# Two score banks become three shared ones, side products get two banks and are evicted one step later

## The chip, the cores and the metric

One core of a Trainium2 chip. The metric is the device time of one execution in microseconds; lower is better. Engine names: PE is TensorE (PEld its weight loads), DVE is VectorE, ACT is ScalarE, POOL is GpSimd, SP is SyncE, which here only issues DMAs.

## The reference

16 sequences of 1024 tokens pass one layer. The parts that matter:

```python
h = tok_ref(x)      # embedding, 128x128 projection, 6 gated convolutions (3 taps), projection
# differential attention, 8 heads of 16 channels:
attn1 = softmax(q1 k1^T / 4);  attn2 = softmax(q2 k2^T / 4)
gate_in = window_stats(attn1), window_stats(attn2)  # windows of 4 rows: mean, std(ddof=1), max, min
alpha = sigmoid(relu(relu(gate_in gw1 + gb1) gw2 + gb2) gw3 + gb3)
h = h + (alpha attn1 + (1 - alpha) attn2) v Wo
# feed-forward on layernorm(h): normalised once more inside, attn_w, then one expert per
# sequence (fc1, gelu, fc2), next projection, gelu
h = h + ffn_ref(layernorm(h))
```

The score matrices are 1024x1024, 16 of them (8 heads, two attentions) for each sequence; row maximum, row minimum and sum of squares of every row feed the window statistics.

## The kernel before

Sixteen bodies, one for each sequence, run in a loop over groups of eight. A body has 128 steps (STEPS); a unit (one head of one attention) takes 8 of them, so step n works on unit n // 8, row tile n % 8. The engines run through the steps in a fixed order, each on its own, tied by semaphores:

- PE: scores(n) (two 512-column halves into ps_s), weighted(n) (exps times v into ps_o), scores_t(n) (the transposed scores of 12 steps earlier into ps_t), then the side products that the plan puts into step n, each into a bank of ps_w.
- DVE: row_max(n) (L726, reads ps_s, writes neg_s and the row maximum), the unit's collection of ps_o if there is one, row_min(n-1) (L734), then the side tasks of the step.
- ACT: exp_t(n) (L594, reads ps_t), the side tasks of the step (evictions of ps_w among them), squares(n) (L587, reads neg_s).
- POOL: only side tasks, in the order of the plan. SP: DMA issues in a hand-written order.

The side work of the sequence before (attention output, gate, layer norms, experts) and of the sequence after (embedding, convolutions, projections for q, k, v) is cut into tasks; plan() puts each into a step, with at most one side product per step. COST is PE's price of a task, POOL_COST that of POOL in tenths of a microsecond, STEP_WEIGHT what POOL works off per step, GAP and SPREAD the least distance to the task before. A task of engine X is done when its last instruction raises side_X; later tasks wait for counts of that semaphore, and every POOL task also waits for the POOL task before it (wait_own).

PSUM has 8 banks. Before: ps_s four (two tiles of two banks, tile n in pair n % 2, free again after row_max(n-2)), ps_t two, ps_o one, ps_w one. A side product waits until the product before it is evicted, and is evicted in its own step: ACT after exp_t(n), DVE after row_min(n-1).

Three chains around the change. msplit j (POOL, 4 small instructions in step 8j-2) splits the row maxima of a unit; mrow j (DVE, at the end of step 8j) waits for it, and DVE's row_max(8j+1) stands behind mrow. snap (POOL, step 16, 11.3 us) takes the statistics; unit 2's collection on DVE in step 21 waits for its end. qk (POOL) splits q and k into three bf16 parts; load_unit on SP then copies the parts of a head into qst and kst, twelve DMAs of 32 KB, and scores of the unit's first step waits for all of them (s_ring). After the last body a tail without scores does the side work of the last sequence, one task after another.

## Time and profile before

| | us |
|---|---|
| runs before | 5776.51, 5781.32, 5792.61 (median 5781.32) |
| the profiled execution | 5777.35, its span 5775.5 |
| prologue, up to the first row_max | 138.2 |
| first to last of 16 body starts | 5182.1 (15 bodies, mean 345.5) |
| last body and tail | 455.2 |
| PE busy | 5177.0 (90%) |
| ACT busy | 5196.2 (90%) |
| DVE busy | 5109.5 (88%) |
| POOL busy | 2454.1 (42%) |

Three engines are busy for about nine tenths of the span. The timeline can be cut by body and by step: row_max (neg_s<-ps_s on DVE, L726) occurs once in each of the 2048 steps, so the distance between two of its starts is the length of a step. In the rows of a timeline the first number is the start, the second the duration, both in us; neighbouring instructions of an engine overlap by about 0.1 us in these records, so prices are read from start to start.

### The profile page before, as it was taken

How to read it: one execution, taken by the hardware profiler on the slowest of the kernel's cores; microseconds unless marked ns; L12 is line 12 of the kernel's file. 1: busy time of each engine (PE TensorE's matmuls, PEld its weight loads, DVE VectorE, ACT ScalarE, POOL GpSimd, SP SyncE). 2: the span in 40 equal slices, each digit the busy share in tenths (PEclk: the TensorE clock that was granted, in tenths of full speed). 3: DMA queues.
4: the chain of work that ended last, by engine and by line, in shares of the span. 5: the costliest groups of instructions: out<-in, count | busy, mean ns of one | idle time of the engine just before them, and what ended most of it. 6: DMA issues, size and time to landing. Idle time of an engine off the chain costs nothing.

```text
span 5775.5 us, 120393 instructions
## 1 busy us (share of the span) xinstructions
PE 5177.0 (90%) x33798; PEld 2429.7 (42%) x33798; DVE 5109.5 (88%) x7715; ACT 5196.2 (90%) x7903; POOL 2454.1 (42%) x4439
## 2 busy tenths in 40 slices
PE   6998989899898998989889898998989899898995
PEld 4443434344343443434334343443434344343442
DVE  1989899898999989899898999989899898989983
ACT  2999999999999999999989999999999999999994
POOL 6525344352533525344352534525344352534523
PEclk8999999999999999999999999999999999999997
DMA  1001010010101001010010101001010010101000
GB/s 35 23 20 31 20 32 20 22 28 19 31 20 32 19 19 32 18 32 21 22 29 21 31 19 31 20 19 32 18 32 21 22 28 21 32 19 30 21 22 14
DMA packets 164931, 140.83 MB, mean 24 GB/s; under 512 B 89196, under 2 KB 108268, under 8 KB 164140
## 3 DMA queue, kind: packets, MB, share of 16 engines
q1 hardware_dynamic: 159100, 124.09, 9.3%
q0 software_dynamic: 4352, 8.92, 0.7%
q8 instruction: 289, 4.73, 0.3%
q14 instruction: 374, 3.06, 0.2%
q10 hardware_dynamic: 816, 0.02, 0.0%
HBM read 21.26 MB, written 8.91 MB: 5 GB/s over the span
## 4 chain that ended last, share of the span: by engine, by line
PE 41%; ACT 21%; issue 17%; POOL 10%; DVE 8%; SPq 2%; DMA 1%; ACTq 1%; POOLq 1%; DVEq 0%
PE ps_w L395 18%; PE ps_t L395 9%; ACT junk L587 9%; PE ps_o L395 7%; ACT exps L594 6%; PE ps_s L395 6%; DVE neg_s L726 3%; ACT hpre L598 2%; SPq L336 2%; DVE rowmin L734 1%; DVE bn L746 1%; POOL part L881 1%; POOL ctmp L1013 1%; POOL part L1015 1%; ACT stage L598 1%
## 5 line engine op out<-in xcount | busy, mean ns | idle before, releaser
L726 DVE TENSOR_SCALAR_CACHE_REDUCE neg_s<-ps_s 128x1024 f32<-128x1024 f32 x2048 | 2492.4, 1217 | 389.8 <-PE ps_s L395 338.3
L734 DVE TENSOR_REDUCE rowmin<-neg_s 128x1 f32<-128x1024 f32 x2049 | 2479.4, 1210 | 0.0
L587 ACT ACTIVATE junk<-neg_s,negmax 128x1024 bf16<-128x1024 f32 x2048 | 2357.9, 1151 | 112.8 <-DVE neg_s L726 106.4
L594 ACT ACTIVATE exps<-ps_t 128x1024 f32<-128x1024 f32 x2060 | 2116.0, 1027 | 179.7 <-PE ps_t L395 174.6
L395 PE MATMUL ps_t<-qst,kst 99*128 99x512 bf16 x4120 | 1274.4, 392 | 235.8 <-ACT exps L594 232.7
L395 PE MATMUL ps_o<-exps,v_cur 128*32 128x256 f32 x16512 | 1351.2, 400 | 143.8 <-DVE o_raw L742 120.8
L395 PE MATMUL ps_s<-kst,qst 96*128 96x512 bf16 x4096 | 1255.3, 388 | 67.3 <-DMA kst<-part 59.0
L395 PE MATMUL ps_w<-xc,cw 128*128 128x256 f32 x4704 | 1158.0, 382 | 3.7 <-DVE z L799 2.7
L395 PEld LDWEIGHTS ps_w<-xc,cw 128*128 128x128 f32 x4704 | 888.8, 190 | 221.2 <-DVE z L799 10.6
L395 PEld LDWEIGHTS ps_o<-exps,v_cur 128*32 128x32 f32 x16512 | 329.0, 109 | 1055.5 <-issue 643.0
L881 POOL TENSOR_SCALAR ctmp<-ug 128x256 f32<-128x256 f32 x408 | 165.8, 406 | 1331.4 <-ACT ug L663 1312.1
L395 PEld LDWEIGHTS ps_t<-qst,kst 99*128 99x128 bf16 x4120 | 236.4, 97 | 1148.1 <-issue 595.7
L395 PEld LDWEIGHTS ps_s<-kst,qst 96*128 96x128 bf16 x4096 | 397.0, 100 | 507.6 <-issue 198.1
L881 POOL TENSOR_SCALAR mparts<-negmax 128x8 bf16<-128x8 f32 x256 | 52.2, 204 | 866.0 <-DVE neg_s L726 826.4
L587 ACT ACTIVATION_READ_ACCUMULATOR junk<-neg_s,negmax 128x1 f32 x2048 | 412.1, 201 | 0.0
L1001 POOL TENSOR_TENSOR ctmp<-ctmp,va 128x256 f32<-128x256 f32 x408 | 298.0, 730 | 33.9
L1002 POOL TENSOR_TENSOR ctmp<-ctmp,xc 128x256 f32<-128x256 f32 x408 | 279.4, 685 | 32.0
L663 ACT ACTIVATE ug<-ps_w,cb_half 128x256 f32<-128x256 f32 x392 | 186.9, 477 | 65.1 <-PE ps_w L395 64.4
L598 ACT ACTIVATE va<-ps_w,cb 128x256 f32<-128x256 f32 x392 | 185.7, 474 | 63.6 <-PE ps_w L395 46.7
L395 PE MATMUL ps_w<-hpre,fc2s 128*128 128x512 f32 x264 | 163.6, 745 | 62.5 <-ACT hpre L643 62.5
L881 POOL TENSOR_SCALAR xc<-ctmp 128x256 f32<-128x256 f32 x408 | 167.6, 411 | 67.0 <-POOL ctmp L1002 67.0
L726 DVE DVE_READ_ACCUMULATOR neg_s<-ps_s 128x1 f32 x2048 | 170.2, 83 | 0.0
(181 smaller groups left out, 3932.8 us busy)
## 6 DMA issues: line engine op xcount, KB each, us to landing
qst<-part SPq DMA_DIRECT2D x1542, 32.0 KB, 2.0
kst<-part SPq DMA_DIRECT2D x1542, 32.0 KB, 2.0
qst<-mrow SPq DMA_DIRECT2D x1028, 1.5 KB
out_dram<-z SPq DMA_DIRECT2D x17, 512.0 KB, 3.2
fc1s<-in_fc_w SPq DMA_DIRECT2D x17, 256.0 KB
fc2s<-in_fc_w SPq DMA_DIRECT2D x17, 256.0 KB
cw<-in_conv_w SPq DMA_DIRECT2D x1, 2304.0 KB
odif<-in_table,idx POOLq DMA_INDIRECT x136
```

The source lines that it names most:

```text
L336: sp.dma_start(dst[HD * g:HD * g + HD, r, :], part[HD * h:HD * h + HD, a, w, c, :])\
L395: return nc.tensor.matmul(dst, lhs, rhs, start=start, stop=stop, **kw)
L587: nc.scalar.activation(junk[:, n % 2, :], neg_s[:, n % SLOTS_S, :], ACT.Exp, scale=-1.0, bias=negmax[:, r, t:t + 1], accum_out=sumsq[:, r, ...
L594: nc.scalar.activation(exps[:, n % RING, :], ps_t[:, :, :].rearrange("p c q -> p (c q)"), ACT.Exp, scale=0.5).then_inc(s_exp, 1)
L598: return nc.scalar.activation(dst, src, ACT.Identity, **kw)
L663: last = nc.scalar.activation(ug[:, c % 2, :], bank[:, CH:2 * CH], ACT.Tanh, scale=0.5, bias=cb_half[:, 2 * l + 1:2 * l + 2])
L726: nc.vector.tensor_scalar(neg_s[:, n % SLOTS_S, :], ps_s[:, n % 2, :], -1.0, None, ALU.mult, ALU.min, accum_out=negmax[:, r, t:t + 1]).the ...
L734: nc.vector.tensor_reduce(rowmin[:, r, t:t + 1], neg_s[:, m % SLOTS_S, :], axis=AX, op=ALU.max, negate=True).then_inc(s_min, 1)
L746: last = nc.vector.bn_stats(bn[:, t, :], src[:, t, :])
L881: return nc.gpsimd.tensor_scalar(*args)
L1001: chain(i, tt(ctmp[:, 1, :], ctmp[:, 0, :], va[:, c % 2, :], ALU.mult))
L1002: chain(i, tt(ctmp[:, 2, :], ctmp[:, 1, :], x_in, ALU.add))
```

## The change

- PSUM: ps_s has three banks for two tiles. Tile n lies in banks n % 2 and n % 2 + 1, so the middle bank belongs to both. The half in the outer bank is written first and waits for row_max(n-2) as before, the half in the middle bank waits for row_max(n-1). ps_w has two banks, taken in turn; a product waits for the eviction of the last but one.
- Eviction one step later: ACT and DVE do the evictions of step n in step n+1, ACT right after exp_t(n+1), DVE between row_max(n+1) and row_min(n). The first half of fc2 is excepted.
- std: two Sqrt activations of ACT become eight POOL instructions (pow 0.5, 128x16 elements each), eight tasks in the plan; win waits for the last of them.
- ln3: the moments of x2 on DVE are gone (8 bn_stats, 8 bn_aggr); POOL works out the factor from the variance of ln2 (three small instructions and a pow) and does one 128x1024 multiplication; the subtraction is gone.
- loads: six DMAs per unit for twelve (1, 2 or 3 copies of 16 rows in each); the three for q wait only for the q parts, the three for k for the k parts.
- plan: snap is priced 115 (80), ln3 50 (66), each std 30; STEP_WEIGHT is 25 (27); a convolution may be placed up to a backlog of 50 (27). Within a step evicted tasks stand last.

The order that plan() then gives, from step 16 (conva/convg l c shortened to a/g l.c; the step number ahead):

```text
before: 16 mrow2 snap; 18 g0.1; 19 a0.2; 20 g0.2; 21 unit2 std; 22 a0.3 msplit3; 23 win; 24 mrow3 g0.3;
 25 hid1; 26 a1.0; 27 hid2; 28 g1.0; 29 unit3 logit; 30 a1.1 msplit4; 31 g1.1; 32 mrow4 alpha; 33 a1.2;
 34 g1.2; 35 a1.3; 36-37 attT; 38 g1.3 msplit5; 39-40 wo; 41 ln2; 43-47 a2.0 to a2.2; 48 ln3; ...
 80 gelu1 fc2; 108 ln1 gelu2; 116, 118, 120, 122 qk; 123-124 v
after:  16 mrow2 snap; 19 g0.1; 20 a0.2; 21 unit2 std0 g0.2; 22 msplit3 a0.3; 23 std1; 24 mrow3 g0.3;
 25 std2; 26 a1.0; 27 std3 g1.0; 28 a1.1; 29 unit3 std4 g1.1; 30 msplit4 a1.2; 31 std5 g1.2;
 32 mrow4 a1.3; 33 std6 g1.3; 34 a2.0; 35 std7; 36 g2.0; 37 unit4 a2.1; 38 msplit5 win; 39 g2.1;
 40 mrow5 hid1; 41 a2.2; 42 hid2; 43 g2.2; 44 logit; 48 alpha; 57 ln2; 64 mrow8 ln3 g4.1; ...
 96 gelu1 fc2; 106 ln1 gelu2; 114, 116, 118, 120 qk; 121-122 v
```

The core of the diff:

```diff
@@ -40,8 +40,8 @@
-Q_PART = (0, 0, 0, 1, 1, 2)
-K_PART = (0, 1, 2, 0, 1, 0)
+RUNS = ((0, 3), (3, 2), (5, 1))
+LOADS = 2 * len(RUNS)
...
@@ -58,16 +58,17 @@
-POST = ([("snap",), ("std",), ("win",), ("hid1",), ("hid2",), ("logit",), ("alpha",)] + two("attT") + two("wo")
+STD = [("std", k) for k in range(U // 2)]
+POST = ([("snap",)] + STD + [("win",), ("hid1",), ("hid2",), ("logit",), ("alpha",)] + two("attT") + two("wo")
...
-    "std": ("act",),
+    "std": ("pool",),
...
-    "ln3": ("dve", "pool"), "nT": ("pe", "act"), "attw": ("pe", "act"), "fc1": ("pe", "act"), "gelu1": ("act",),
+    "ln3": ("pool",), "nT": ("pe", "act"), "attw": ("pe", "act"), "fc1": ("pe", "act"), "gelu1": ("act",),
...
@@ -78,17 +79,17 @@
-POOL_COST = {"msplit": 8, "unit": 5, "qk": 35, "convg": 23, "gather": 85, "snap": 80, "alpha": 46, "hcopy": 20,
-             "ln1": 66, "ln2": 66, "ln3": 66, "gelu2": 24, "vcopy": 15}
-STEP_WEIGHT = 27
...
-GAP = {("std",): 5, ("win",): 2, ("hid1",): 2, ("hid2",): 2, ("logit",): 2, ("alpha",): 2, ("attT", 0): 4,
+POOL_COST = {"msplit": 8, "unit": 5, "qk": 35, "convg": 23, "gather": 85, "snap": 115, "alpha": 46, "hcopy": 20,
+             "ln1": 66, "ln2": 66, "ln3": 50, "std": 30, "gelu2": 24, "vcopy": 15}
+STEP_WEIGHT = 25
...
+GAP = {("std", 0): 5, ("win",): 3, ("hid1",): 2, ("hid2",): 2, ("logit",): 2, ("alpha",): 2, ("attT", 0): 4,
...
-SPREAD = {"attw": 2, "fc1": 2}
+SPREAD = {"attw": 2, "fc1": 2, "std": 2}
...
@@ -122,9 +123,9 @@
-                if task[0] in ("conva", "convg") and behind > STEP_WEIGHT:
+                if task[0] in ("conva", "convg") and behind > 2 * STEP_WEIGHT:
...
-                if stage is pre and any(t[0] in ("gelu1", "gelu2", "std") for t in at[n]):
+                if stage is pre and any(t[0] in ("gelu1", "gelu2") for t in at[n]):
...
@@ -136,8 +137,14 @@
-        at[n].sort(key=lambda task: task[0] != "unit")
+        at[n].sort(key=lambda task: (task[0] != "unit", task[0] in READER))
+    assert not any(is_late(task) for task in at[STEPS - 1])
...
+def is_late(task):
...
+    return task[0] in READER and task != ("fc2", 0)
...
@@ -176,10 +183,10 @@
-        ps_s = ctx.enter_context(nc.psum_tensor("ps_s", [P, 2, L], F32))
+        ps_s = ctx.enter_context(nc.psum_tensor("ps_s", [P, 3, 512], F32))
...
-        ps_w = ctx.enter_context(nc.psum_tensor("ps_w", [P, 512], F32))
+        ps_w = ctx.enter_context(nc.psum_tensor("ps_w", [P, 2, 512], F32))
...
@@ -281,15 +289,18 @@
-            if phase == "body" or task not in users:
-                return ps_w[:, :]
-            return (ps_w[:, :], ps_t[:, 0, :], ps_t[:, 1, :])[users.index(task) % 3]
+            if task not in users:
+                return ps_w[:, 0, :]
+            at = users.index(task)
+            if phase == "body":
+                return ps_w[:, at % 2, :]
+            return (ps_w[:, 0, :], ps_t[:, 0, :], ps_t[:, 1, :])[at % 3]
...
-            at = users.index(task) - (1 if phase == "body" else 3)
+            at = users.index(task) - (2 if phase == "body" else 3)
...
@@ -328,13 +339,20 @@
-            def load_unit(u):
+            def load_q(u):
...
-                for g in range(NPART):
-                    for dst, w, c in ((qst, 0, Q_PART[g]), (kst, 1, K_PART[g])):
-                        sp.dma_start(dst[HD * g:HD * g + HD, r, :], part[HD * h:HD * h + HD, a, w, c, :])\
-                          .then_inc(s_ring[r], 16)
+                for c, (g, count) in enumerate(RUNS):
+                    src = part[HD * h:HD * h + HD, a, 0, c, :]
+                    sp.dma_start(qst[HD * g:HD * (g + count), r, :],
+                                 src.unsqueeze(1).to_broadcast([HD, count, L])).then_inc(s_ring[r], 16)
...
+            def load_k(u):
...
+                a, h, r = u // H, u % H, u % RING
+                for g, count in RUNS:
+                    sp.dma_start(kst[HD * g:HD * (g + count), r, :], part[HD * h:HD * h + HD, a, 1, 0:count, :])\
+                      .then_inc(s_ring[r], 16)
...
@@ -360,8 +378,10 @@
-            wait_side(sp, "pre", 0, "pool", QK[0][-1])
-            load_unit(0)
+            wait_side(sp, "pre", 0, "pool", QK[0][1])
+            load_q(0)
+            wait_side(sp, "pre", 0, "pool", QK[0][3])
+            load_k(0)
...
@@ -377,10 +397,11 @@
-                        if j + 1 in (U // 2, U):
-                            wait_side(sp, "body", i, "pool", QK[(j + 1) % U // H][-1])
-                            settle()
-                        load_unit((j + 1) % U)
+                        for part_of, load in ((1, load_q), (3, load_k)):
+                            if j + 1 in (U // 2, U):
+                                wait_side(sp, "body", i, "pool", QK[(j + 1) % U // H][part_of])
+                                settle()
+                            load((j + 1) % U)
...
@@ -398,10 +419,11 @@
-                    pe.wait_ge(s_ring[u % RING], i * (4 * 12 * 16) + 12 * 16 * (u // RING + 1))
-                pe.wait_ge(s_max, i * STEPS + n + 1)
-                for c in range(2):
-                    last = mm(ps_s[:, n % 2, 512 * c:512 * c + 512], qst[0:KSC, u % RING, P * t:P * t + P],
+                    pe.wait_ge(s_ring[u % RING], i * (4 * LOADS * 16) + LOADS * 16 * (u // RING + 1))
+                first = n % 2
+                for k, c in enumerate((first, 1 - first)):
+                    pe.wait_ge(s_max, i * STEPS + n + 1 + k)
+                    last = mm(ps_s[:, n % 2 + c, :], qst[0:KSC, u % RING, P * t:P * t + P],
...
@@ -452,7 +474,7 @@
-                    w("act", ("std",))
+                    w("pool", STD[-1])
...
@@ -612,13 +634,6 @@
-                elif kind == "std":
-                    w("pool", ("snap",))
-                    for a in range(2):
-                        last = nc.scalar.activation(
-                            gin[:, :, :, 4 * a + 1].rearrange("p t h -> p h t"),
-                            gtmp[:, 3, U * T // 2 * a:U * T // 2 * (a + 1)].rearrange("p (h t) -> p h t", h=H),
-                            ACT.Sqrt)
...
@@ -693,8 +708,11 @@
+                        for tk in STEP[n - 1] if n else ():
+                            if is_late(tk):
+                                task("body", i, tk)
...
-                            if tk != ("fc2", 0):
+                            if tk[0] not in READER:
...
@@ -723,7 +741,8 @@
-                nc.vector.tensor_scalar(neg_s[:, n % SLOTS_S, :], ps_s[:, n % 2, :], -1.0, None, ALU.mult, ALU.min,
+                nc.vector.tensor_scalar(neg_s[:, n % SLOTS_S, :].rearrange("p (c k) -> p c k", c=2),
+                                        ps_s[:, n % 2:n % 2 + 2, :], -1.0, None, ALU.mult, ALU.min,
...
@@ -789,9 +808,6 @@
-                elif kind == "ln3":
-                    w("pool", ("ln2",))
-                    last = moments(i, x2, 1)
...
@@ -842,19 +859,22 @@
-            pos.update(loop=True, base=pos["n"], n=0, per=3)
+            pos.update(loop=True, base=pos["n"], n=0, per=2)
...
+                        for tk in STEP[n - 1] if n else ():
+                            if is_late(tk):
+                                task("body", i, tk)
...
-                            if tk[0] != "unit":
+                            if tk[0] != "unit" and tk[0] not in READER:
...
@@ -972,6 +992,11 @@
+                elif kind == "std":
+                    a, h = tk[1] // (H // 2), tk[1] % (H // 2) * 2
+                    last = tt(gin[:, :, h:h + 2, 4 * a + 1].rearrange("p t h -> p h t"),
+                              gtmp[:, 3, T * (H * a + h):T * (H * a + h + 2)].rearrange("p (h t) -> p h t", h=2),
+                              half_pow[:, :, :], ALU.pow)
...
@@ -985,9 +1010,12 @@
-                    w("dve", tk)
...
-                    last = normalise(i, att, x2, 1)
+                    chain(i, tt(rstd[:, 1, :], mv[:, 0, :, 1], rstd[:, 0, :], ALU.mult))
+                    chain(i, tt(rstd[:, 1, :], rstd[:, 1, :], rstd[:, 0, :], ALU.mult))
+                    chain(i, ts(rstd[:, 1, :], rstd[:, 1, :], 1.0, EPS, ALU.mult, ALU.add))
+                    chain(i, tt(rstd[:, 1, :], rstd[:, 1, :], rs_pow[:, :], ALU.pow))
+                    last = tt(att[:, :, :], x2[:, :, :], rstd[:, 1, :].unsqueeze(2).to_broadcast([P, T, P]), ALU.mult)
...
```

## Rows read from the trace of the kernel before

**Rows 1.** The page's first section: busy time, share of the span and instructions of each engine

```profile
PE 5177.0 (90%) x33798; PEld 2429.7 (42%) x33798; DVE 5109.5 (88%) x7715; ACT 5196.2 (90%) x7903; POOL 2454.1 (42%) x4439
```

**Rows 2.** The page's costliest groups: busy, mean ns, idle before and its releaser

```profile
L726 DVE TENSOR_SCALAR_CACHE_REDUCE neg_s<-ps_s 128x1024 f32<-128x1024 f32 x2048 | 2492.4, 1217 | 389.8 <-PE ps_s L395 338.3
...
L663 ACT ACTIVATE ug<-ps_w,cb_half 128x256 f32<-128x256 f32 x392 | 186.9, 477 | 65.1 <-PE ps_w L395 64.4
```

**Rows 3.** Timeline, DVE: row_max of step 0, first body and last body

```profile
138.23 1.23 DVE L726 TENSOR_SCALAR_CACHE_REDUCE neg_s<-ps_s 128x1024 f32<-128x1024 f32 x1 [20.00 <-PE ps_s L395]
...
5320.35 1.22 DVE L726 TENSOR_SCALAR_CACHE_REDUCE neg_s<-ps_s 128x1024 f32<-128x1024 f32 x1 [0.54 <-PE ps_s L395]
```

**Rows 4.** Timeline of the ninth body's last steps (126, 127), up to the next body

```profile
3240.08 0.60 PE L395 MATMUL ps_t<-qst,kst 99*128 99x512 bf16 x2
...
3240.47 1.21 DVE L726 TENSOR_SCALAR_CACHE_REDUCE neg_s<-ps_s 128x1024 f32<-128x1024 f32 x1
3240.53 0.60 PE L395 MATMUL ps_s<-kst,qst 96*128 96x512 bf16 x2
...
3242.75 1.22 DVE L726 TENSOR_SCALAR_CACHE_REDUCE neg_s<-ps_s 128x1024 f32<-128x1024 f32 x1
...
3244.70 1.03 PE L395 MATMUL ps_s<-kst,qst 96*128 96x512 bf16 x2 [2.23 <-DMA kst<-part]
```

**Rows 5.** Timeline of the ninth body, PE in steps 67 (fc1) and 68 (convolution)

```profile
3078.48 0.60 PE L395 MATMUL ps_t<-qst,kst 99*128 99x512 bf16 x2
...
3079.79 0.60 PE L395 MATMUL ps_s<-kst,qst 96*128 96x512 bf16 x2
...
3080.89 0.60 PE L395 MATMUL ps_t<-qst,kst 99*128 99x512 bf16 x2
...
3082.63 0.60 PE L395 MATMUL ps_s<-kst,qst 96*128 96x512 bf16 x2
```

**Rows 6.** Timeline of the ninth body, steps 17 to 24: DVE and POOL around snap's end

```profile
2943.93 1.16 DVE L726 TENSOR_SCALAR_CACHE_REDUCE neg_s<-ps_s 128x1024 f32<-128x1024 f32 x1
...
2954.84 0.60 POOL L974 TENSOR_TENSOR gin<-gtmp,recip 128x64 f32<-128x64 f32 x2
...
2955.56 0.45 DVE L742 STREAM_TRANSPOSE o_raw<-ps_o 128x256 f32<-128x256 f32 x1 [1.32 <-POOL gin L974]
...
2957.03 1.21 DVE L726 TENSOR_SCALAR_CACHE_REDUCE neg_s<-ps_s 128x1024 f32<-128x1024 f32 x1
...
2958.40 0.41 POOL L881 TENSOR_SCALAR ctmp<-ug 128x256 f32<-128x256 f32 x1 [0.23 <-POOL xc L881]
...
2961.21 0.20 POOL L894 TENSOR_TENSOR dif_all<-rowmin,negmax 128x8 f32<-128x8 f32 x1 [0.30 <-POOL xc L881]
...
2962.93 0.20 POOL L931 TENSOR_TENSOR mparts<-mrest,mparts 128x8 bf16<-128x8 f32 x1
```

**Rows 7.** The groups by line and shape: pow, a small instruction, the table load for Sqrt

```profile
L900 POOL TENSOR_TENSOR rstd<-rstd,rs_pow 128x8 f32<-128x8 f32 x51 | 84.5, 1658 | 4.3
...
L618 ACT ACT_TABLE_LOAD x17 | 21.8, 1283 | 0.3
...
L881 POOL TENSOR_SCALAR rstd<-mv 128x8 f32<-128x8 f32 x51 | 10.1, 198 | 345.5 <-DVE mv L750 345.5
```

**Rows 8.** Timeline of the ninth body, end of step 8 on DVE

```profile
2923.67 0.21 DVE L766 STREAM_TRANSPOSE mrow<-mparts 128x32 bf16<-128x32 bf16 x1 [2.58 <-POOL mparts L931]
```

**Rows 9.** Timeline of the ninth body: first row_max behind the gelu step (80)

```profile
3123.25 1.23 DVE L726 TENSOR_SCALAR_CACHE_REDUCE neg_s<-ps_s 128x1024 f32<-128x1024 f32 x1 [8.80 <-PE ps_s L395]
```

**Rows 10.** Timelines of prologue and tail: first scores; std; second norm in the tail

```profile
137.16 1.03 PE L395 MATMUL ps_s<-kst,qst 96*128 96x512 bf16 x2 [19.66 <-DMA kst<-part]
...
5699.54 0.46 ACT L618 ACTIVATE gin<-gtmp 128x64 f32<-128x64 f32 x2 [12.30 <-POOL gin L974]
...
5734.10 0.20 POOL L881 TENSOR_SCALAR rstd<-mv 128x8 f32<-128x8 f32 x1 [2.57 <-DVE mv L750]
...
5736.10 1.90 POOL L901 TENSOR_TENSOR odif<-x,mv 128x1024 f32<-128x1024 f32 x1
```

6 lines of the change are left out of this document (4 added, 2 removed).

## The prediction

> **What bounds the kernel now.** I read the busy shares first: three engines stand at 88 to 90% [rows 1], so no single one explains the time. Next the costliest groups: DVE's row_max idles 390 us, 338 of them for PE's scores, so DVE and PE take turns as the bound [rows 2]. Then the timeline, cut at the row_max starts. Between the first and the sixteenth body start lie 5182.1 us [rows 3], 345.5 per body. Averaging each of the 128 step lengths over the bodies (2048 row_max starts, the first and the last body in rows 3), nearly every step has one of a few lengths.
>
> A step with no side work takes 2.27 or 2.28 us: DVE goes from row_max to row_max without idling, while PE has time left [rows 4]. PE's own price of a step: 1.10 from scores to scores_t, then 0.45 to the next scores if there is no product, 1.31 with one of fc1, 1.74 with a convolution half [rows 4, 5]. So PE needs 1.54 bare, 2.41 with fc1, 2.84 with a convolution half, and where convolutions or fc1 stand in every step these are the step lengths: PE-bound. The side pieces of DVE (collections, layer norm moments, evictions) add 22.1 us to 127 x 2.27.
>
> This gives a tally for any plan: each step costs what DVE needs; PE may fall 0.7 us behind for nothing, and what it falls behind beyond that is added. 0.7 is from the new kernel: the middle bank is free when row_max(n-1) ends, 1.14 us after its start; wait and half a tile bring the scores to 1.56, and DVE wants them at 2.27. In the old kernel PE has a whole spare tile, but ACT's eviction in the product's own step takes the room back. The same 0.7 fits it: DVE's needs 310.4, tally 326.0, measured 334.2, all without the gelu step. The missing 8.2 I can name, but for 0.7: unit 2 waits 1.35 for snap [rows 6], mrow for POOL in steps 8, 112 and 120 (1.05, 1.2 and 0.9 on average; in the body shown 2.58 in step 8 [rows 8]), the next body's scores for their loads about 1.5 with what follows [rows 4], win 0.7, smaller ones 0.9. The gelu step is 11.3: 8.80 of idle and 2.5 of work [rows 9].
>
> **The change part by part.** *The plan.* I walked the planner's loop with its new numbers; the front part shows the order. DVE's needs fall by 2.3, the moments of ln3, to 308.1. But the tally of the new plan is 325.9 against 326.0: convolutions stand closer, 16 in steps 17 to 38 for 13, and the two long norm steps in which PE caught up are one now. The gain on DVE is lost to PE. Worth 0.
>
> *Three score banks.* PE loses the tile it could write ahead; that is in the 0.7. In a bare step scores are ready 0.7 before DVE wants them, so there it costs nothing. Bounds: 0, and 0.7 at each of some five places where the old kernel ran through several convolutions at 2.27 (after steps 17, 41 and 48), 3.5 a body. I take 0, since the tally has it already.
>
> *Two side banks and late eviction.* ACT idled for unfinished products, 64 us before ug [rows 2], and before the other evictions too. Those waits go. In PE-bound steps they cost nothing, and the tally without them fits the old kernel, so I take 0 beyond the wait of win. Bounds: 0 and 7 a body, all of them.
>
> *std on POOL*, the term that decides. pow on 8 columns took 1.66, a small instruction 0.20 [rows 7]. If the surplus goes by columns it is 0.18 each, and 16 columns take 3.1; with the 0.25 between tasks, 3.35. Eight are 27 us on an engine that is half idle over the body, but not here. POOL's prices from the trace: snap ends 11.5 after row_max(17), a convolution takes 2.7 to 2.8 from start to start, unit and msplit together 1.9 [rows 6]. POOL's queue in plan order, us after row_max(17): convg 0.1 from 11.7, unit 2 from 14.5, std 0 from 15.3, convg 0.2 from 18.65, msplit 3 from 21.45 to 22.6. mrow 3 waits for it at the end of step 24, which DVE reaches at 19.9 (step 22 starts at 13.1 as now [rows 6], then three of 2.27). DVE stands 2.7, and behind mrow stand row_max(25) and so squares and the scores of 26. Then std 1, convg 0.3, std 2, std 3, convg 1.0, unit 3, std 4, convg 1.1 and msplit 4 end at 46.4, where PE's pace brings mrow 4 to 44.3; std 5, convg 1.2, std 6, convg 1.3 and std 7 end at 61.95. win on PE waits for that, with all of PE's queue behind it: 1.15 for win and 0.6 for the scores put row_max(39) at 63.8. The tally without POOL gives 56.9, so the queue costs 6.9 a body. Now the stretch takes 58.9. Lower bound: a pow with the same 1.66 however many columns; then std is 1.9, msplit 3 ends at 21.2, the rest never waits: 1.9 with unit 2's wait for snap. On ACT the Sqrt's table load (1.28 [rows 7]), the load back and two short activations go, about 3 us a body; ACT isn't late there, so only win's wait in step 23 is saved.
>
> *Loads.* The row of 12 DMAs issues one each 0.63 us; the next body's first scores stood 2.23 for it and PE came back at half clock, 1.03 for 0.60 [rows 4]. With three left behind the last k part, and the qk tasks two steps earlier, they land some 4 us ahead. Of the waits outside steps 17 to 38 there remain 1.2 in the first steps (the gather and four qk tasks still fill POOL before msplit 1) and 0.3 after ln1. Should a DMA of three copies take longer, 4 us hide it; without that cover it is late second for second. In the prologue nine issues less behind the last part: -5.7 of the 19.66 [rows 10].
>
> *Clock.* After idle PE falls to 1.2 GHz now and then: 6 of 16 bodies show it in step 43 or 44, after the 2.3 us of ln2, 1.6 us each time, 0.6 over all. Two new idle places (steps 24 and 38) for one old: +0.6.
>
> *Tail.* Everything is serial. std now ends 0.46 after POOL [rows 10]; eight pows take 26.8, +26. ln3's wait for moments (2.57 [rows 10]) and a pass of 1.9 go, 0.9 of small steps come: -3.6. Together +22.4; with a flat pow +11.
>
> **Sum.** A body: 325.9 + 1.2 + 6.9 + 0.3 + 11.3 + 0.6 = 346.2, 0.7 over 345.5. Sixteen: +11. 5777.35 + 11 - 5.7 + 22.4 = 5805. The profiled execution lies 4 us under the median, inside the spread of the runs; I keep 5805.
>
> **Rivals.** *Pow is flat.* Then steps 17 to 38 take 58.8, a body 340.6, 16 x -4.9 = -78; prologue -5.7, tail +11: 5704, the faster side. For it: a POOL instruction's start counts, 8 to 64 columns of an ordinary one differ by 0.1. Against: 1.46 us over an ordinary instruction of the same size looks like work by element, and the plan's own price is 30, where its others (snap 115, ln2 66) are near what the trace shows. It decides from a std under about 2.4 us. Chance 0.2, half-way cases in it.
>
> The Trainium skill, GPSIMD Engine Reference, section 3.1, puts elementwise work at about 2.6 cycles per element; by that eight more columns would cost next to nothing, which is this rival's time. The trace's 1.66 for 8 columns already speaks of something else than that rate.
>
> *Late eviction gives more.* If half of ACT's waits for products were on the path after all, 3.5 a body come back, some 57 us: 5748. For it: each of these waits delays squares and the next exp_t, and scores_t of the next step stands behind that. Against: the tally explains the old steps without them. Chance 0.2.
>
> *PE's clock.* If both new stands drop the clock in every body, and convolutions follow at 1.2 GHz, each costs what 1.30 + 1.54 more would, less the slack, some 2.3: 346.2 + 4 a body, 5870. For it: 2.23 of idle did it at the end of every body, as in the one shown [rows 4]. Against: after step 8's stand of 2.58 [rows 8] the next scores were at full clock. Chance 0.15. Lost write-ahead (3.5 a body at most) would end there too.
>
> *The change doesn't do what it says*: the next body still waits for its loads. Then 1.5 a body come back, +24, inside the range.
>
> **How the numbers follow.** The forecast, with 5775 to 5840 of its own (std 3.0 to 3.5 is -10 to +20 us, the loads +24), has 0.45; flat pow 0.2, late eviction 0.2, clock 0.15. Reaching to all but the outer parts of flat pow and clock, the range is 5715 to 5860. Differences under 0.3% (17 us) can't be told from none. Of the forecast's 0.45 about 0.27 is beyond 17 us slower and 0.18 within; clock is slower; late eviction faster but for 0.04; flat pow faster. Faster 0.36, same 0.22, slower 0.42.
>
> **What would show it.** std's mean in the group of POOL pows (3.1, or 1.7). The step from row_max(24) to row_max(25): 5.1, with mrow idle for POOL's mparts; 3.6 if pow is flat. Row_max(17) to (39): 63.8. ACT's wait before ug near zero. No DMA row before the scores of a body's first step. Steps with a convolution still 2.84, bare ones 2.27; if bare steps or lone convolutions are longer, the 0.7 of room is wrong, and so is the prediction, as it is if POOL isn't full from step 21 to 38.

## The result, and the profile after

| | before | after |
|---|---|---|
| median of the runs | 5781.66 us (5776.51 to 5792.61) | 5834.93 us (5827.91 to 5837.84) |
| ratio | 1 | 1.0090, 95% interval 1.0074 to 1.0106 |
| profiled execution | 5775.5 us, clock 0.963 | 5834.6 us, clock 0.950 |

The kernel became slower by 0.9%, 53 us, where +0.4% was forecast. The kernel moved the way that was forecast and its time lies in the range, but of the measured slowdown the sum explains less than half. The busy shares and the costliest groups of the profile after (line, engine, operation, shapes, count, then busy time, mean ns of one, then idle time before it and its releaser; for [rows 1, 2]):

```profile
PE 5287.0 (91%) x33798; PEld 2463.3 (42%) x33798; DVE 5080.7 (87%) x7444; ACT 5114.6 (88%) x7835; POOL 2817.4 (48%) x4592
...
L744 DVE TENSOR_SCALAR_CACHE_REDUCE neg_s<-ps_s 128x1024 f32<-128x1024 f32 x2048 | 2489.9, 1216 | 474.7 <-PE ps_s L416 400.5
L616 ACT ACTIVATE exps<-ps_t 128x1024 f32<-128x1024 f32 x2060 | 2124.1, 1031 | 471.5 <-PE ps_t L416 456.5
...
L416 PE MATMUL ps_s<-kst,qst 96*128 96x512 bf16 x4096 | 1373.5, 394 | 335.2 <-DVE neg_s L744 308.2
...
L997 POOL TENSOR_TENSOR gin<-gtmp,half_pow 128x16 f32<-128x16 f32 x136 | 398.1, 2927 | 11.1
```

row_max idles 475 us where it idled 390 [rows 2], and the third row is new: PE itself now stands 335 us ahead of its scores, 308 of them released by DVE's row_max. That is the shared bank. It isn't all added, though. PE's waits have moved: before, it stood ahead of scores_t, for ACT's exps. The first two rows are of the kernel before, the third is of after:

```profile
L395 PE MATMUL ps_t<-qst,kst 99*128 99x512 bf16 x4120 | 1274.4, 392 | 235.8 <-ACT exps L594 232.7
L395 PE MATMUL ps_s<-kst,qst 96*128 96x512 bf16 x4096 | 1255.3, 388 | 67.3 <-DMA kst<-part 59.0
L416 PE MATMUL ps_t<-qst,kst 99*128 99x512 bf16 x4120 | 1292.7, 397 | 19.1 <-ACT exps L616 13.1
```

Together the two waits are 303 us before and 354 after. The last row of the first fence is the pow: 2.93 us for 16 columns, 398 us of GpSimd. The groups of ACT show that the evictions do go off ACT's path as meant; ug waited 64 us for PE [rows 2]:

```profile
L678 ACT ACTIVATE ug<-ps_w,cb_half 128x256 f32<-128x256 f32 x392 | 185.2, 472 | 2.8 <-PE ps_w L416 2.7
```

Next the cut at the row_max starts, the first of the first body and the first of the last (timeline of DVE: start, duration, then the instruction and the idle time before it), for [rows 3]:

```profile
131.60 1.22 DVE L744 TENSOR_SCALAR_CACHE_REDUCE neg_s<-ps_s 128x1024 f32<-128x1024 f32 x1 [14.65 <-PE ps_s L416]
5351.71 1.22 DVE L744 TENSOR_SCALAR_CACHE_REDUCE neg_s<-ps_s 128x1024 f32<-128x1024 f32 x1 [0.45 <-PE ps_s L416]
```

(5351.71 - 131.60) / 15 = 348.01 a body, for 345.47 [rows 3]. The last row_max of all starts at 5698.20, and at 5661.38 before. So the difference of the two spans, 59.1 us, falls into these parts:

| us | measured | forecast |
|---|---|---|
| up to the first row_max | -6.6 | -5.7 |
| sixteen bodies | 15 x 2.54 + 5.5 = +43.6 | +11 |
| behind the last row_max | +22.2 | +22.4 |

So the ends are as forecast and the miss lies in the body. The next table has the mean length of its stretches over fifteen bodies. The forecast's column is its tally, divided by stretch afterwards; the 0.6 for the clock isn't in it. Beside it stands `banks_old`, the experiment below that gives the change its old banks back:

| steps | before | forecast | after | banks_old |
|---|---|---|---|---|
| 0 to 16 | 43.7 | 42.5 | 43.7 | 42.9 |
| 17 to 38 | 58.9 | 63.8 | 61.6 | 62.8 |
| 39 to 95 | 159.0, gelu step in it | 149.9 | 152.6 | 149.7 |
| 96 | 2.8 | 11.3 | 10.9 | 10.7 |
| 97 to 127 | 81.1 | 78.2 | 79.2 | 78.9 |

Outside steps 17 to 38 the forecast was 281.9 and the kernel took 286.4; inside them it was 63.8 for 61.6. Two errors of opposite sign.

### The profile page after: what moved, and what is told of

The parts are those of the page before. It is cut to its first block and busy times, and to the rows that moved or that the text cites. A ratio compares the mean times of both kernels' runs of the same rounds, so it can differ in the third digit from the quotient of the medians.

```text
span 5834.6 us, 119048 instructions
## 1 busy us (share of the span) xinstructions
PE 5287.0 (91%) x33798; PEld 2463.3 (42%) x33798; DVE 5080.7 (87%) x7444; ACT 5114.6 (88%) x7835; POOL 2817.4 (48%) x4592
## 5 line engine op out<-in xcount | busy, mean ns | idle before, releaser
L616 ACT ACTIVATE exps<-ps_t 128x1024 f32<-128x1024 f32 x2060 | 2124.1, 1031 | 471.5 <-PE ps_t L416 456.5
L609 ACT ACTIVATE junk<-neg_s,negmax 128x1024 bf16<-128x1024 f32 x2048 | 2373.7, 1159 | 61.6 <-DVE neg_s L744 61.0
L416 PE MATMUL ps_s<-kst,qst 96*128 96x512 bf16 x4096 | 1373.5, 394 | 335.2 <-DVE neg_s L744 308.2
L416 PE MATMUL ps_o<-exps,v_cur 128*32 128x256 f32 x16512 | 1373.6, 406 | 28.4 <-POOL v_cur L1054 20.3
L416 PE MATMUL ps_t<-qst,kst 99*128 99x512 bf16 x4120 | 1292.7, 397 | 19.1 <-ACT exps L616 13.1
L416 PE MATMUL ps_w<-xc,cw 128*128 128x256 f32 x4704 | 1175.0, 386 | 0.0
L416 PEld LDWEIGHTS ps_w<-xc,cw 128*128 128x128 f32 x4704 | 906.4, 193 | 212.5 <-issue 10.9
L609 ACT ACTIVATION_READ_ACCUMULATOR junk<-neg_s,negmax 128x1 f32 x2048 | 429.3, 210 | 0.0
L997 POOL TENSOR_TENSOR gin<-gtmp,half_pow 128x16 f32<-128x16 f32 x136 | 398.1, 2927 | 11.1
L901 POOL TENSOR_SCALAR part<-stage 128x512 bf16<-128x512 f32 x132 | 81.8, 619 | 250.1 <-ACT stage L620 235.9
```

The source lines that it names most:

```text
L416: return nc.tensor.matmul(dst, lhs, rhs, start=start, stop=stop, **kw)
L609: nc.scalar.activation(junk[:, n % 2, :], neg_s[:, n % SLOTS_S, :], ACT.Exp, scale=-1.0, bias=negmax[:, r, t:t + 1], accum_out=sumsq[:, r, ...
L616: nc.scalar.activation(exps[:, n % RING, :], ps_t[:, :, :].rearrange("p c q -> p (c q)"), ACT.Exp, scale=0.5).then_inc(s_exp, 1)
L901: return nc.gpsimd.tensor_scalar(*args)
L997: last = tt(gin[:, :, h:h + 2, 4 * a + 1].rearrange("p t h -> p h t"), gtmp[:, 3, T * (H * a + h):T * (H * a + h + 2)].rearrange("p (h t) ...
```

## The experiments

All are compared with the kernel before, run on the same chip beside them. "Body" is the time from one body's first row_max to the next one's, as above; "clock" is the mean granted clock of the profiled execution, as a share of 2.4 GHz.

| run | median us | ratio to before, 95% interval | body | clock |
|---|---|---|---|---|
| after | 5834.93 | 1.0090 (1.0074 to 1.0106) | 348.0 | 0.950 |
| std_mul | 5768.86 | 0.9975 (0.9965 to 0.9985) | 345.3 | 0.954 |
| banks_old | 5790.36 | 1.0014 (1.0005 to 1.0024) | 345.0 | 0.964 |
| fill | 5825.66 | 1.0074 (1.0057 to 1.0091) | 347.5 | 0.971 |
| std_mul_fill | 5736.92 | 0.9921 (0.9905 to 0.9938) | 343.0 | 0.979 |
| shared_only | 5826.83 | 1.0078 (1.0061 to 1.0095) | 347.1 | 0.952 |
| own_step | 5828.29 | 1.0091 (1.0074 to 1.0108) | 347.4 | 0.947 |
| std_mul_banks_old | 5695.23 | 0.9850 (0.9834 to 0.9867) | 340.1 | 0.967 |
| b_banks | 5989.05 | 1.0353 (1.0336 to 1.0370) | 358.9 | 0.934 |
| b_banks_fill | 5956.67 | 1.0308 (1.0291 to 1.0326) | 356.4 | 0.960 |
| b_ln3_loads | 5735.71 | 0.9919 (0.9903 to 0.9936) | 342.6 | 0.968 |
| b_ln3_loads_fill | 5785.45 | 1.0005 (0.9995 to 1.0015) | 346.3 | 0.971 |
| new_plan_act | 5719.41 | 0.9891 (0.9875 to 0.9908) | 342.0 | 0.968 |

**The queue of pows.** `std_mul` keeps the plan and the eight tasks and makes each of them an ordinary multiplication; the square root is left out.

```diff
-                              half_pow[:, :, :], ALU.pow)
+                              half_pow[:, :, :], ALU.mult)
```

> The changed kernel with the eight pows of std turned into multiplications of the same shape, which leaves the square root out; all else, the plan too, stays. Theory queue: GpSimd's queue between snap and win sets steps 17 to 38. A multiplication takes about 0.2 us for 2.93, so msplit 3, msplit 4 and win wait no more: the stretch falls from 61.6 us to 58 to 59, a body from 348.0 to about 345, and the tail by 8 x 2.7 = 22: some 65 to 75 us less, 5760 to 5770. Rival clock: the stretch is long because TensorE falls to 1.2 GHz in steps 18, 19 and 26; then these steps stay at 3.6 and 3.1 us on average and only the step of mrow 3 and win's change: stretch 60 or more, the tail's 22 us go all the same, in all 35 to 50 us less, 5785 to 5800.

Steps 17 to 38 fell from 61.6 to 58.7, as the queue theory has it, and the kernel by 66 us: 2.7 a body and the tail's 25. Step 24 of the ninth body shows the mechanism, first in after (DVE, then POOL):

```profile
2976.01 1.21 DVE L744 TENSOR_SCALAR_CACHE_REDUCE neg_s<-ps_s 128x1024 f32<-128x1024 f32 x1
2980.01 0.21 DVE L785 STREAM_TRANSPOSE mrow<-mparts 128x32 bf16<-128x32 bf16 x1 [1.66 <-POOL mparts L951]
2980.15 1.22 DVE L744 TENSOR_SCALAR_CACHE_REDUCE neg_s<-ps_s 128x1024 f32<-128x1024 f32 x1
...
2972.75 2.95 POOL L997 TENSOR_TENSOR gin<-gtmp,half_pow 128x16 f32<-128x16 f32 x1
2975.94 0.40 POOL L901 TENSOR_SCALAR ctmp<-ug 128x256 f32<-128x256 f32 x1 [0.24 <-POOL gin L997]
...
2979.69 0.20 POOL L951 TENSOR_TENSOR mparts<-mrest,mparts 128x8 bf16<-128x8 f32 x1
2979.97 2.93 POOL L997 TENSOR_TENSOR gin<-gtmp,half_pow 128x16 f32<-128x16 f32 x1
```

POOL goes from a pow to a convolution half to mparts with gaps of 0.3 at most, and DVE stands 1.66 for it; row_max(25) comes 4.14 after row_max(24). In `std_mul` the same step has no wait and takes 2.39 (DVE's timeline, and the row of the multiplication among POOL's groups):

```profile
2959.31 1.21 DVE L744 TENSOR_SCALAR_CACHE_REDUCE neg_s<-ps_s 128x1024 f32<-128x1024 f32 x1
2961.58 0.20 DVE L785 STREAM_TRANSPOSE mrow<-mparts 128x32 bf16<-128x32 bf16 x1
2961.70 1.18 DVE L744 TENSOR_SCALAR_CACHE_REDUCE neg_s<-ps_s 128x1024 f32<-128x1024 f32 x1
```
```profile
L997 POOL TENSOR_TENSOR gin<-gtmp,half_pow 128x16 f32<-128x16 f32 x136 | 30.8, 226 | 11.1
```

The mean lengths of steps 19 and 59 stayed at 3.5 and 3.6, though, so part of what is long is not the queue.

**The banks.** `banks_old` keeps the rest of the change and goes back to four score banks (two for each tile), one side bank and the eviction in the product's own step:

```diff
-        ps_s = ctx.enter_context(nc.psum_tensor("ps_s", [P, 3, 512], F32))
+        ps_s = ctx.enter_context(nc.psum_tensor("ps_s", [P, 2, L], F32))
-        ps_w = ctx.enter_context(nc.psum_tensor("ps_w", [P, 2, 512], F32))
+        ps_w = ctx.enter_context(nc.psum_tensor("ps_w", [P, 512], F32))
...
-                        for tk in STEP[n - 1] if n else ():
-                            if is_late(tk):
-                                task("body", i, tk)
```

> The changed kernel with the banks and the eviction of before (two score tiles of two banks, one bank for side products, eviction in the product's own step); its plan, pows, norm and loads stay. Theory clock: the half that waits for row_max(n-1) holds TensorE idle in one piece in each step without a product, and the clock falls in steps 18, 19, 26, 59 and 126 of many bodies; with the old banks these halvings go, 3 to 4 us a body, 50 to 60 us less than the changed kernel: about 5780. Rival: late eviction and the second side bank are worth their waits, so undoing them costs 50 us or more: 5885. If the tally's room of 0.7 us is the same for both, as the prediction took it, and the clock plays no part, no difference within 15 us.

44 us came back (ratio 1.0014 for 1.0090), 3.0 a body, near the first theory's time. None of it comes from steps 17 to 38, which grew to 62.8. Steps 59 to 62 took 2.27, 2.27, 2.60 and 2.27 on average, for 3.48, 2.85, 2.84 and 2.84 in after. PE in steps 58 and 59 of the ninth body, behind the norm ln2 of step 57, in after:

```profile
3070.25 1.46 PE L416 MATMUL ps_w<-xc,cw 128*128 128x256 f32 x6
3071.55 0.38 PE L416 MATMUL ps_s<-kst,qst 96*128 96x512 bf16 x1
3074.06 0.39 PE L416 MATMUL ps_s<-kst,qst 96*128 96x512 bf16 x1 [2.13 <-DVE neg_s L744]
...
3074.95 0.77 PE L416 MATMUL ps_t<-qst,kst 99*128 99x512 bf16 x2
3075.51 2.77 PE L416 MATMUL ps_w<-xc,cw 128*128 128x256 f32 x6
3078.07 0.90 PE L416 MATMUL ps_s<-kst,qst 96*128 96x512 bf16 x2
```

One half of the scores is written, and then PE stands 2.13 for row_max(58), the reader of the middle bank. The matmuls behind it show the granted clock's lower level, 1.2 GHz: the six of the convolution half take 2.77 for the 1.46 just before, the scores 0.90 for 0.60. DVE has to wait 1.60 for them. The same place in `banks_old`:

```profile
3052.88 0.60 PE L413 MATMUL ps_s<-kst,qst 96*128 96x512 bf16 x2
3053.41 0.64 PE L413 MATMUL ps_o<-exps,v_cur 128*32 128x256 f32 x8
3055.12 0.59 PE L413 MATMUL ps_t<-qst,kst 99*128 99x512 bf16 x2 [1.07 <-ACT exps L612]
3055.55 1.49 PE L413 MATMUL ps_w<-xc,cw 128*128 128x256 f32 x6
```

Both halves are written at once, PE's stand is shorter and comes between other work, and the clock stays at 2.4 GHz. PE doesn't stand less over the whole run: in `banks_old` it waits 346 us ahead of scores_t, more than the 335 ahead of the scores in after. But it waits with a whole tile written ahead:

```profile
L413 PE MATMUL ps_t<-qst,kst 99*128 99x512 bf16 x4120 | 1272.9, 391 | 346.1 <-ACT exps L612 344.7
```

By the traces' records of the granted clock over fifteen bodies, the lower level covers 20.3 us a body before, 19.0 in `banks_old` and 29.2 in after.

**Only the clock?** `fill` leaves the banks of the change and gives PE idle bf16 matmuls in the steps without a product, whose results nobody reads: two in each (none around fc2), but eleven in ln2's step, nine in ln1's, five in snap's.

```diff
+                for _ in range(2 + sum({'ln2': 9, 'ln1': 7, 'snap': 3}.get(k[0], 0) for k in STEP[n])):
+                    mm(bank, qst[0:KSC, u % RING, P * t:P * t + P], kst[0:KSC, u % RING, 0:512])
```

> The changed kernel with idle work on TensorE: in each step without a product two more matrix products of a score half's size (0.5 us in all), nine in the steps of the two norms and five in the step of snap, into the free side bank, read by nobody; none around fc2. Nothing is left out. Theory clock: TensorE stays at 2.4 GHz, steps 10, 59, 108, 127 lose their 0.3 to 1.2 us, about 3 us a body, 45 us less: 5790; in steps 17 to 38 GpSimd's queue keeps what the clock gives back. Rival: the clock isn't the cause; the added products only take TensorE's room (0.7 us), steps after bare ones grow by up to 0.5 us each: 5850 or more.

The steps behind the long norm step went as the clock theory says (59: 2.28, 60: 2.84); the scores' second half now waits 0.54, at full clock (timeline of PE, `fill`):

```profile
3068.97 0.39 PE L416 MATMUL ps_s<-kst,qst 96*128 96x512 bf16 x1 [0.54 <-DVE neg_s L766]
...
3070.30 1.46 PE L416 MATMUL ps_w<-xc,cw 128*128 128x256 f32 x6
3071.60 0.60 PE L416 MATMUL ps_s<-kst,qst 96*128 96x512 bf16 x2
```

The time at the lower level fell from 29.2 us a body to 12.6, less than before and in `banks_old`. But the kernel gained only 9 us, a difference that the two intervals don't separate, and steps 39 to 95 only 0.9 of the 2.9 that `banks_old` gains. Most of the other 2.0 is plain room: step 60 is 2.84 with the shared bank at full clock, and 2.27 with own banks. Some is the price of the idle matmuls themselves, since a few steps grew (39 from 2.91 to 3.07, 67 from 2.34 to 2.53, 96 from 10.9 to 11.3). What they gain is therefore the least that the clock is worth. `std_mul_fill` takes the queue away as well (both edits above, again without the square root):

> Both: multiplications for the pows of std (the square root is left out) and the idle work on TensorE. If queue and clock both hold, steps 17 to 38 fall to the tally's 57 to 58 us, a body to about 341 and the tail by 22: about 5700, and more than the two single gains added in steps 17 to 38. If the clock isn't a cause, no better than with the multiplications alone.

It came to 0.9921, 343.0 a body, for 345.3 of `std_mul`. So the clock is worth at least 2.3 a body where the queue doesn't lie over it, and at least 0.5 where it does. The expected 5700 was too low: it put the whole room down to the clock.

**Which part of the banks?** `shared_only` is `banks_old` with the three score banks, `own_step` has the second side bank too; with the late eviction added that is the change.

```diff
 shared_only, against the change:
-        ps_w = ctx.enter_context(nc.psum_tensor("ps_w", [P, 2, 512], F32))
+        ps_w = ctx.enter_context(nc.psum_tensor("ps_w", [P, 512], F32))
 shared_only and own_step:
-                        for tk in STEP[n - 1] if n else ():
-                            if is_late(tk):
-                                task("body", i, tk)
                         for tk in STEP[n]:
-                            if tk[0] not in READER:
+                            if tk != ("fc2", 0):
```

> The changed kernel with one side bank and eviction in the product's own step as before, but the three shared score banks kept (seven banks in use). Against the run with all banks of before (5790 us, body 345.0) it shows the price of the sharing alone, against the changed kernel (5835, body 348.0) the worth of the late eviction. Theory room: the sharing takes about 2 us a body of write-ahead in steps 39 to 95 (runs of convolutions at 2.27 us turn into 2.84) and 1 us of clock; and ACT then also waits for products in their own step with no room to hide it: 5850 to 5880. Rival: late eviction costs as such and the sharing little: 5790 to 5810.

> The change with the eviction in the product's own step again; three score banks and two side banks stay. With shared score banks, one side bank and eviction in the own step the body was 347.1, with two side banks and late eviction 348.0. Theory (the late place of the eviction costs it: ACT's eviction stands ahead of the squares of the next step, POOL's convolution and its successors come a step later; the second bank is worth little): about 347.0 a body, 5820 to 5830. Rival (a second side bank in use lets PE write further ahead and so stand in a longer piece, wherever the eviction lies): about 348, 5832 to 5842. If the second bank helps while late eviction hurts more: under 346.5, 5815 or less.

`shared_only` missed both of its theories. `own_step` is in the first theory's range by its time, 5828.3, and between the first two by its body, 347.4. Sharing costs 2.1 of the 3.0 a body (345.0 to 347.1, 36 us by the medians). In `shared_only` step 59 takes 2.27, and steps 39 to 95 show no lower clock at all; still they take 151.2 for the 149.7 of `banks_old`, with steps 60 and 62 at 2.84 for 2.27. That is the price of the lost room without the clock. What the second bank and the late eviction add, 0.3 and 0.6 a body in the profiled executions, is 8 us and inside the intervals of the three ratios (1.0078, 1.0091, 1.0090). None of them shows a gain from evicting later. ACT's groups in `own_step`, which differs from after by the late eviction alone, show where the waits went:

```profile
L616 ACT ACTIVATE exps<-ps_t 128x1024 f32<-128x1024 f32 x2060 | 2135.9, 1037 | 238.8 <-PE ps_t L416 232.8
L678 ACT ACTIVATE ug<-ps_w,cb_half 128x256 f32<-128x256 f32 x392 | 187.4, 478 | 78.5 <-PE ps_w L416 77.7
```

Evicting later took ug's wait from 78.5 us to 2.8 and raised that of exps from 238.8 to 471.5.

**The same two suspects on the old kernel.** `b_banks` puts the banks and the late eviction, nothing else, on the kernel before.

> The kernel before with only the banks and the late eviction of the change (old plan, std on ACT, twelve loads, ln3 with its moments). Theory room: the old plan has more places where several convolutions run at 2.27 us (steps 18 to 20 and 50 to 53 and 43 to 46), so here the sharing costs as much or more: 3 us a body, 5830. If ACT's waits for products (64 us before ug) were worth something on this plan, less: 5780.

It cost 3.5% (1.0353), 13.4 a body, over four times the 3 that were expected. In the old plan the norm step stands right ahead of convolutions (43 and 50: 4.35 and 4.70 for 2.27), win in step 23 takes 5.89 for 3.50, and step 127, at whose end the next body's loads land, 6.59 for 3.26. In the ninth body POOL is through with the last q and k part 13.7 us after row_max(120), for 11.3 before. That fits the later eviction of the qk results, which no run isolates. PE's timeline in steps 41 to 43 and at the end of the ninth body:

```profile
3122.32 0.38 PE L404 MATMUL ps_s<-kst,qst 96*128 96x512 bf16 x1
3126.34 0.39 PE L404 MATMUL ps_s<-kst,qst 96*128 96x512 bf16 x1 [3.63 <-DVE neg_s L739]
3126.66 1.03 PE L404 MATMUL ps_o<-exps,v_cur 128*32 128x256 f32 x8
3127.62 1.03 PE L404 MATMUL ps_t<-qst,kst 99*128 99x512 bf16 x2
3128.45 2.32 PE L404 MATMUL ps_w<-xc,cw 128*128 128x256 f32 x6
...
3364.38 1.03 PE L404 MATMUL ps_s<-kst,qst 96*128 96x512 bf16 x2 [3.82 <-DMA kst<-part]
```

The first five rows are the pattern of step 59 again, larger: one stand of 3.63, then 1.03 where weighted and scores_t take 0.64 and 0.60 at full clock, and 2.32 for the 1.46 of the convolution half. The last is the DMA wait of [rows 4], 3.82 for 2.23. With idle matmuls (`b_banks_fill`, the filler of `fill`):

> The kernel before with the change's banks and late eviction (5989 us, body 358.9), plus idle matrix products on TensorE in steps without a product: two, eleven in the step of ln2, nine in those of ln1 and five in snap's; read by nobody. Theory clock: in steps 18, 43 and 50 TensorE stood 2 to 3.6 us for row_max before the second half, fell to 1.2 GHz and did the convolution behind it there; with the pauses of ln2 and snap filled, steps 18 and 43 fall from 3.7 and 4.4 to under 2.9 us, 3 us a body, 50 us or more in all: about 5930; step 50, behind ln3, gets no more than the two products and changes less. Rival: these steps are long for want of room, not for the clock: then they stay above 3.5 us and the time at 5980 or more.

Steps 18 and 43 fell to 2.27 and 2.38, step 50 only to 4.17, and by the ratios 26 us came back of the 204. On the old plan, too, the idle matmuls give back the smaller share; here as well that is the least that the clock is worth.

**The parts that gain.** `b_ln3_loads` is the kernel before with ln3 without its moments and with the six loads:

> The kernel before with two parts of the change that touch neither banks nor plan: ln3 without its moments on DVE, and six loads per unit. Step 48 falls from 4.67 to 2.4 us, but TensorE loses the pause in which it caught up, so one of the 2.3 us comes back in steps 50 to 56; the next body's scores no longer wait for loads (1.0 to 1.5 us a body); prologue 6 and tail 4 us less. Sum: 2 to 3.5 us a body and 10: 5725 to 5745. If TensorE takes back all of the 2.3 us: 5755.

0.9919, as expected. Step 48, ln3's, fell from 4.67 to 2.41, though steps 51 to 53 gave 0.2, 0.6 and 0.2 back, and the first row_max came at 133.1 for 138.2. `b_ln3_loads_fill` adds the idle matmuls:

> The kernel before with ln3 without moments, six loads (5736 us) and the idle matrix products. The old banks leave few falls of the clock (steps 0, 1, 43, 110, 111), worth about 0.7 us a body: 5720 to 5730 if the products cost nothing; if they take the room of steps behind them, 5745 or more.

It lost all of it again (1.0005): steps 23 and 24 went from 3.41 and 2.87 to 4.46 and 4.17. With one side bank an idle matmul has to wait for the eviction ahead of it; what it then delays stays open.

`new_plan_act` takes the planner's new numbers, ln3 and the loads, and keeps the old banks and ACT's std (one task, two Sqrt activations). The order that the planner then gives isn't that of the change but close to the old one, with ln3 in step 48 and the gelu step at 80:

```diff
-STD = [("std", k) for k in range(U // 2)]
+STD = [("std", 0)]
...
-    "std": ("pool",),
+    "std": ("act",),
```

> All parts of the change but the banks with late eviction and the pows: std is one task on ACT, the planner has the new prices and orders by them. Against banks-of-before with pows (5790 us) it shows the price of the pows: GpSimd's queue no longer sets steps 17 to 38, and the tail loses 25: from the run with multiplications and old banks, about 5695. ACT's Sqrt costs step 21 to 24 up to 1.5 us a body, and the order differs (close to the old plan's): 5710 to 5735. If the new prices are worth something beside the other parts, it is below 5736, the old plan with ln3 and loads.

5719.41 us, 0.9891: faster than both kernels, and the fastest of the versions that compute everything. Its busy shares and the groups that answer to those of after:

```profile
PE 5147.1 (90%) x33798; PEld 2433.5 (43%) x33798; DVE 5061.4 (89%) x7444; ACT 5196.7 (91%) x7903; POOL 2420.9 (42%) x4456
...
L744 DVE TENSOR_SCALAR_CACHE_REDUCE neg_s<-ps_s 128x1024 f32<-128x1024 f32 x2048 | 2489.3, 1215 | 398.0 <-PE ps_s L413 336.2
...
L612 ACT ACTIVATE exps<-ps_t 128x1024 f32<-128x1024 f32 x2060 | 2112.1, 1025 | 142.5 <-PE ps_t L413 136.7
```

ACT's exps waits 142 us where it waits 471 in after. PE is 140 us less busy with the same 33798 matmuls; part of that is the clock. The new numbers of the planner add little to ln3 and the loads: 0.9891 for the 0.9919 of `b_ln3_loads`, and the two intervals overlap.

Last, the two suspects crossed. `std_mul_banks_old` has both edits (the multiplication for the pow, without the square root, and `banks_old`):

> Banks and eviction of before, and multiplications for the pows of std (the square root is left out). With the pows, the old banks gained nothing in steps 17 to 38 (62.8 us for 61.6), since GpSimd's queue sets that stretch. Theory room under a queue: without the queue the old banks show their room there too, the stretch falls to 55 to 57 us (58.7 with the shared banks), a body to 338 to 339, and the time to about 5670. Rival: the sharing matters only behind a norm (steps 58 to 62); then the stretch stays at 58.5 and the time at 5700 to 5720.

The time came out 25 us above the first theory's and 5 below the rival's range; the stretch from 17 to 38 took 57.4, 0.4 above the first theory's range and 1.1 below the rival's. With it the body's square is complete:

| us a body | old banks | the change's banks | the banks cost |
|---|---|---|---|
| multiplication | 340.1 | 345.3 | 5.2 |
| pow | 345.0 | 348.0 | 3.0 |
| the pow costs | 4.9 | 2.7 | |

Each hides 2.2 of the other. The table of stretches shows where: outside 17 to 38 the banks cost 4.2 even with the pow; inside, where POOL is the bound, they cost nothing. There row_max(25) comes 22.6 after row_max(17) in after, `banks_old` and `fill` alike, however the steps between divide it: the queue sets it, and a shorter step is only waited for later. Why that stretch is in the end even 1.2 shorter with the new banks no run settles.

## Why the prediction was off

**The failed step** is "Three score banks ... I take 0, since the tally has it already". The 0.7 of room was worked out from the new kernel's middle bank, and was then taken for the old kernel too, because the tally met that kernel's total. With one room for both the sum had no difference between them, and its level was that of a kernel with a whole spare tile. Step by step it did not fit the old kernel: behind steps 17, 41 and 48 this ran through several convolutions at 2.27, where the tally charged 2.70 and 2.84, and elsewhere the tally was too cheap. The prediction had seen just those places and had priced them at up to 3.5 a body. With its old banks the changed kernel meets the tally to 0.3 outside steps 17 to 38 (282.2 for 281.9, `banks_old`); with the new ones it stands 4.5 above. The banks cost 3.0 a body, 44 us, near the bound that was given and not the value that was taken. With the 4.2 that they cost outside the queue's stretch, and the 2.2 that this stretch is shorter than forecast, the sum would have been 5805 + 16 x (4.2 - 2.2) = 5837. That is bookkeeping after the fact and no test, and the 0.6 for the clock, which is part of the 4.2, is in it twice.

Part of the near miss is luck. The two errors in the body, +67 and -35 us over sixteen bodies, have opposite signs, and 17 of the 28 us of slowdown that were forecast come from the ends, which were right.

**The clock**, sized 0.6 a body for steps 24 and 38, is a share of the same step. In after it is low above all in steps 18, 19, 26 and 59 and in 106 to 110 and 125 to 127, and in the first four of these behind a stand in which one half of the scores is out and the other waits. Not every such stand does it: 0.61, one step ahead of the 2.13, did not. It is worth at least 0.5 a body beneath the queue and 2.3 without it. The waits for semaphores by engine and releaser (total us, times, longest) show the change; [rows 4] has PE in the old kernel waiting for DMA instead:

```profile
PEld ps_s L416 <- DVE neg_s L744: 705.5, 906, 4.1
...
PE ps_s L416 <- DVE neg_s L744: 308.2, 354, 3.4
...
DVE mrow L785 <- POOL mparts L951: 50.5, 39, 3.7
```

The clock rival was named for the stands of steps 24 and 38: the first is followed by the lower clock in step 26 of 9 bodies of 16, the second in none, and the 4 a body that it priced did not come. What the prediction held against it was a misreading: the 2.58 of step 8 [rows 8] is a wait of DVE. PE worked through it and stood 0.79 behind it, ahead of a scores_t:

```profile
2927.27 0.60 PE L395 MATMUL ps_t<-qst,kst 99*128 99x512 bf16 x2 [0.79 <-ACT exps L594]
```

The Trainium skill, TensorE: Matmul & The Clock Gate, section "A second HAM failure mode: psum-queue depth-cycling", describes a kernel whose PE falls idle for short times between groups of matmuls as it cycles through PSUM banks, and changes clock again and again. That is the kind of fault that the shared bank brings, though the page has no shared bank. Here the trace agrees in kind, with 29.2 us a body at the lower level for 20.3; but with the level's time cut to 12.6 (`fill`) only 0.5 of the banks' 3.0 came back.

**The queue** was right in kind and too large: 61.6 measured for 63.8. The pow took 2.93, not 3.1, which is worth 8 x 0.17 = 1.4 at the end of the walk (62.4, against 62.8 in `banks_old` and 61.6 in after). Against a kernel in which std costs next to nothing it is worth 4.9 a body with the old banks (6.9 was the term), 2.7 with the new. Step 24 is 4.14 in the body shown and 3.73 on average, for 5.1. Step 38 ended as described: win starts when the last pow is through (PE, then POOL, then DVE's next row_max):

```profile
3017.57 1.12 PE L416 MATMUL ps_w<-cst,gin 128*64 128x32 f32 x16
...
3014.21 2.92 POOL L997 TENSOR_TENSOR gin<-gtmp,half_pow 128x16 f32<-128x16 f32 x1
...
3019.26 1.22 DVE L744 TENSOR_SCALAR_CACHE_REDUCE neg_s<-ps_s 128x1024 f32<-128x1024 f32 x1 [0.33 <-PE ps_s L416]
```

**Flat pow** is refuted: 16 columns took 2.93 where 8 took 1.66 [rows 7], 0.16 us for each column more. The Trainium skill, GPSIMD Engine Reference, section 3.1, has elementwise work at about 2.6 cycles an element; an estimate from that has the eight columns more nearly free. The measurement decides, and for pow they are not.

**Late eviction gives more** is refuted by `shared_only` and `own_step`, under shared score banks. ACT's waits for products did go, and came back as a wait of exps. The Trainium skill, Perfetto Trace Analysis, section "Matmuls", advises rotating independent groups of matmuls through different PSUM banks so that evictions overlap the next group. Here a second bank for side products, paid with a score bank, brought no gain (1.0091 with it, 1.0078 without). With own score banks two side banks could not be tried: the four of them, two of ps_t, one of ps_o and two side banks would be nine banks of 512 columns, one more than the eight of the old layout.

**The change doesn't do what it says** is refuted. PE's wait for the loads ahead of its scores was 59.0 us in 16 waits before; in after it is the prologue's one of 14.3. At the end of the ninth body PE waits 0.49 for ACT and not for a DMA:

```profile
3261.65 0.64 PE L416 MATMUL ps_o<-exps,v_cur 128*32 128x256 f32 x8 [0.49 <-ACT exps L616]
3262.66 0.38 PE L416 MATMUL ps_s<-kst,qst 96*128 96x512 bf16 x1
```

**Plan, ln3 and loads**: without the queue the forecast had them at 339.3 a body; the waits for snap and for win that ran inside the queue's stretch, 1.35 and 0.7, are still in a kernel with std on ACT, so 4.1 below the old body. `new_plan_act` measured 3.5 below, though with an order near the old one. `std_mul_banks_old`, which has the change's own order, took 340.1 for the 339.3. **Prologue and tail**: -6.6 for -5.7, and +22.2 for +22.4; the eight pows of the tail stand in a row behind a last small pair:

```profile
5738.05 0.60 POOL L994 TENSOR_TENSOR gin<-gtmp,recip 128x64 f32<-128x64 f32 x2
5738.73 23.89 POOL L997 TENSOR_TENSOR gin<-gtmp,half_pow 128x16 f32<-128x16 f32 x8
```

By ratios the change falls into three: the planner's new numbers, ln3 and loads -1.1%, std on GpSimd with the order that its eight tasks bring +1.2% (1.0014 for 0.9891), banks and late eviction +0.8% (1.0090 for 1.0014).

## What to carry to other kernels

That a slack meets a kernel's total does not show that the kernel has that slack: check it step by step where it decides, and when a change takes away a buffer, put the bound and not zero into the sum. Here a bank shared by two tiles in flight moved the matmul engine's waits to where it has nothing written ahead, and it paid twice, in lost write-ahead and in the clock. The busy engine's total idle time did not show this; the lengths of single steps did. Two costs that lie over each other in one body need the crossed experiment: here each of the two, taken away alone, showed 2.2 a body less than with the other gone.
